# A DiT block, minGRU, Runge-Kutta scan and sparse FFN: the last attention pass by token halves, and the second half's recurrence by time with its later steps on GpSimd

## What is computed

```python
# 1 block: adaLN, 16 heads of 128 (attention inside each sequence of 32 tokens), GELU MLP 256-1024-256
x = x + gate1 * (attention(ln(x) * (1 + scale1) + shift1) @ out_w + out_b)
x = x + gate2 * (gelu((ln(x) * (1 + scale2) + shift2) @ ffn_w1 + b1) @ ffn_w2 + b2)
# 2 minGRU along the 32 tokens of each sequence, in linear form
z = sigmoid(x @ Wz.T + bz); h[t] = (1 - z[t]) * h[t-1] + z[t] * g(x @ Wn.T + bn)[t]; x = x + h
# 3 Runge-Kutta scan, 32 steps, each of four derivatives with tanh(q) @ coupling.T; q starts at cond
# 4 logits = q @ Wr.T; the 4 best of 16 blocks of a 1024-wide hidden layer stay; out = x + W2 gelu(W1 q)
```

## Time and profile before

| | |
|---|---|
| median of 3 runs | 482.5 us (482.31 to 483.1) |
| profiled execution | 482.44 us, of which 480.6 us span from first to last instruction |
| TensorE, weight loads | 467.4 us (97%), 334.8 us (70%) |
| VectorE, ScalarE, GpSimd | 389.3 us (81%), 318.9 us (66%), 48.0 us (10%) |
| chain of work that ended last | TensorE 88%, VectorE 4%, ScalarE 3% |
| last attention pass; LayerNorm 2 to hidden layer | about 176 to 232 us; 232 to 241 us |
| second half's gates to the loop | 291 to 305 us |
| loop | 304.8 to about 469 us |

### The profile page before, as it was taken

One profiled execution on the slowest core, in us unless ns is written; L12 is line 12 of the kernel. 1 busy time (PEld: TensorE's weight loads), 2 busy tenths in 40 slices (PEclk: granted clock), 3 DMA queues, 4 the chain that ended last, 5 costly groups with the idle time before them and its releaser, 6 DMA issues.

```text
span 480.6 us, 13808 instructions
## 1 busy us (share of the span) xinstructions
PE 467.4 (97%) x5271; PEld 334.8 (70%) x5271; DVE 389.3 (81%) x1368; ACT 318.9 (66%) x950; POOL 48.0 (10%) x78
## 2 busy tenths in 40 slices
PE   7999999999999999999899999999999999999997
PEld 4455776557656676568545444788898988989886
DVE  4969895779768899997896997888888888888884
ACT  1677964788477966887476965565665656656563
POOL 3010240223020320223000000000000000000000
PEclk9999999999999999999999999999999999999999
DMA  8992510100201000000000000000000000000000
GB/s 283 419 388 70 135 45 22 62 25 23 66 22 44 22 0 2 0 2 1 1 1 1 0 1 0 3 3 1 0 1 11 12 0 12 0 12 11 1 12 23
DMA packets 10399, 20.85 MB, mean 43 GB/s; under 512 B 1472, under 2 KB 4992, under 8 KB 9728
## 3 DMA queue, kind: packets, MB, share of 16 engines
q1 hardware_dynamic: 9808, 19.89, 12.0%
q10 hardware_dynamic: 560, 0.60, 0.4%
HBM read 19.40 MB, written 1.08 MB: 43 GB/s over the span
## 4 chain that ended last, share of the span: by engine, by line
PE 88%; DVE 4%; ACT 3%; DMA 1%; issue 1%; POOL 1%; SPq 0%; DVEq 0%
PE bank L884 58%; PE score L884 27%; PE spare L884 2%; DMA ao_sb<-xtok 1%; POOL ptx L507 1%; ACT ptx L632 1%; ACT ao_sb L585 1%; DVE drive L1459 1%; ACT x L532 0%; ACT th L810 0%; DVE drive L1463 0%; DVE q_group L2112 0%; DVE tok_stats L1406 0%; DVE acc L1551 0%; DVE drive L1614 0%
## 5 line engine op out<-in xcount | busy, mean ns | idle before, releaser
L884 PE MATMUL bank<-x,pairs_store 128*128 128x512 f16 x384 | 86.3, 379 | 0.5 <-ACT x L532 0.4
L884 PEld LDWEIGHTS bank<-x,pairs_store 128*128 128x128 f16 x384 | 36.9, 98 | 43.4 <-issue 1.4
L507 POOL TENSOR_TENSOR ptx<-pt,ptx 32x256 f16<-32x256 f32 x62 | 43.2, 697 | 176.2 <-ACT ptx L632 172.8
L884 PE MATMUL score<-cub,neg_eye 128*128 128x64 f32 x256 | 55.6, 299 | 0.0
L585 ACT ACTIVATE big<-bank,head_b 128x512 f16<-128x512 f32 x60 | 39.8, 685 | 17.4 <-PE bank L884 17.0
L2026 DVE TENSOR_TENSOR thlo<-th 128x64 f16<-128x64 f32 x128 | 28.8, 225 | 26.0 <-ACT th L811 24.8
L884 PE MATMUL score<-th,coup_part 128*128 128x32 f16 x1024 | 46.2, 177 | 0.9
L884 PE MATMUL bank<-pairs_store,ao_sb 128*128 128x256 f16 x360 | 43.0, 273 | 0.7 <-issue 0.2
L884 PE MATMUL bank<-pairs_store,x 128*128 128x512 f16 x192 | 43.4, 379 | 0.0
L810 ACT ACTIVATE th<-score 128x64 f16<-128x64 f32 x96 | 21.5, 224 | 31.7 <-PE score L884 28.9
L884 PEld LDWEIGHTS bank<-pairs_store,ao_sb 128*128 128x128 f16 x360 | 34.0, 98 | 7.5 <-DVE ao_sb L1652 1.5
(11 more groups left out here) (252 smaller groups left out, 1052.1 us busy)
## 6 DMA issues: line engine op xcount, KB each, us to landing
wqk_sb<-wqk SPq DMA_DIRECT2D x16, 256.0 KB, 2.7
wv_sb<-wv SPq DMA_DIRECT2D x4, 512.0 KB, 5.4
wo_sb<-wo SPq DMA_DIRECT2D x4, 512.0 KB, 4.2
f_sb<-ffn_w SPq DMA_DIRECT2D x2, 1024.0 KB, 14.7
ao_sb<-xtok SPq DMA_DIRECT2D x4, 256.0 KB, 5.8
x_sb<-xT SPq DMA_DIRECT2D x1, 1024.0 KB, 12.5
w_sb<-w1T SPq DMA_DIRECT2D x1, 1024.0 KB, 16.1
w_sb<-w2T SPq DMA_DIRECT2D x1, 1024.0 KB, 16.9
```

Source lines behind the costliest of these rows:

```text
L507: nc.gpsimd.tensor_tensor(ptx[s, 1, :, s], pt[s], ptx[s, 0, :, s], ALU.subtract).then_inc(ptx_ready, 1)
L884: return nc.tensor.matmul(dst, lhsT, rhs, start=start, stop=stop, **kw)
```

## The change

In the last pass the fourth head's softmax, placing and mixing are done per half of the tokens (`half_strips`, `shift_half`, `normalise_half`, `place_high_half`, `mix_half`, on 128 x 128 values each), and TensorE's order becomes: mix_half(2, 0), mix_half(2, 1), (0, 2), mix_half(3, 0), head 2 for c = 0, 1, the SHIFT2 product, head 3 for c = 0, 1, mix_half(3, 1), (0, 3). The heads 2 and 3 for c = 2, 3 come behind `turn_normed(0)`. The unread matmuls there become 4. Because of it `take_heads(2)` and `take_heads(3)` come later in VectorE's stream, `empty_x2(0)` later in ScalarE's, and the banks of the hidden layer's tiles are dealt out anew.

For the second half the time steps are cut into 0 to 7 (EARLY, 128 columns) and 8 to 31 (LATE, 384 columns). VectorE runs the recurrence of the early steps for both ob ahead of the loop. GpSimd computes the late steps' terms (`late_terms`), VectorE scans them in eight pieces of 96 columns in the slots of stages 6 to 13 of iteration 0, and GpSimd adds x and makes the drive pair (`late_pair`). ScalarE makes the late gates of ob = 1 (`late_gates(1)`) just ahead of the loop. 18 unread matmuls become 4, and the sum on TensorE is gone.

The diff, cut to its core:

```diff
 # GpSimd
+                    if i == NQUAD - 1 and j == QUAD - 1:
+                        for h in range(NH):
+                            gs = slice(h * G // 2, (h + 1) * G // 2)
...
+                                nc.gpsimd.tensor_tensor(ptx[s, 1, gs, s], pt[s, gs], ptx[s, 0, gs, s], ALU.subtract
+                                                        ).then_inc(half_placed[h], 1)
-            nc.gpsimd.memset(unit_row, 1.0 / CSCALE).then_inc(unit_ready, 1)
+            def late_terms(ob):
+                z, cand, pos, keep = (late_store[:, ob, w] for w in range(4))
+                use = USE_GRU[1] + ob
+                pool.wait_ge(free[bank_of(use)], count_of(use) + 1)
+                own.step(nc.gpsimd.tensor_scalar(keep, z, -0.5, 0.5, ALU.mult, ALU.add))
+                own.step(nc.gpsimd.tensor_scalar(z, z, 1.0, 0.25, ALU.add, ALU.mult))
+                pool.wait_ge(late_tanh, ob + 1)
+                own.step(nc.gpsimd.tensor_scalar(cand, cand, 0.0, 1.0, ALU.min, ALU.add))
+                use = USE_GRU[1] + 3 - ob
+                pool.wait_ge(free[bank_of(use)], count_of(use) + 1)
+                own.step(nc.gpsimd.tensor_tensor(cand, cand, pos, ALU.add))
+                own.step(nc.gpsimd.tensor_tensor(cand, cand, z, ALU.mult))
+                pool.wait_ge(z_used, KB + ob + 1)
...
+                own.step(nc.gpsimd.tensor_tensor(carry[:, ob], keep, state, ALU.mult))
+                own.step(nc.gpsimd.tensor_tensor(cand, cand, carry[:, ob], ALU.add))
+                nc.gpsimd.memset(keep, 0.0).then_inc(late_ready, 1)
+            def late_pair(ob):
...
+                pool.wait_ge(late_scanned, 4 * (ob + 1))
+                own.step(nc.gpsimd.tensor_tensor(later_steps(drive, ob), steps_of(ob)[:, 2], later_steps(x_sb, ob), ALU.add))
+                own.step(nc.gpsimd.tensor_scalar(shifted_drive, later_steps(drive, ob), c2_shifted[:, ob:ob + 1], None, ALU.add))
+                own.step(nc.gpsimd.tensor_scalar(high, later_steps(drive, ob), c2_shifted[:, ob:ob + 1], None, ALU.add))
+                nc.gpsimd.tensor_tensor(low, shifted_drive, high, ALU.subtract).then_inc(late_split, 1)
 # ScalarE, last pass
+                    copy_half(0)
+                    copy_half(1)
+                    place_high(2)
+                    exps_half(0)
+                    exps_half(1)
+                    place_high_half(0)
+                    empty_pv(2)
+                    empty_pv(3, [0])
+                    place_high_half(1)
+                    mlp_highs(5, 7)
+                    empty_pv(3, [1])
+                    mlp_highs(7, 8)
...
+            act.wait_ge(first_heads_out, 1)
             normalise_x2(0)
+            x1_high(NH)
+            act.wait_ge(last_full, 1)
             empty_x2(0)
-            x1_high(NH)
 # ScalarE, second half
+            early_gates(0)
+            early_gates(1)
+            late_gates(0)
+            drive_bias(2, 3, EARLY)
+            drive_bias(3, 4, EARLY)
             tanh_of(q_group[:, :, UNROLL - 1], Q_UNIT[3])
-            drive_bias(3, 5, slice(0, UNROLL))
-            drive_bias(3, 5, slice(UNROLL, T))
+            late_gates(1)
 # TensorE
+                    mix_half(2, 0)
+                    mix_half(2, 1)
+                    out_project(0, 2, [0, 1])
+                    mix_half(3, 0)
+                    out_project(1, 0, [2])
+                    out_project(1, 1, [2])
+                    pe.wait_ge(ada2_ready, 4)
+                    ada_late(SHIFT2, spare)
+                    out_project(1, 0, [3])
+                    out_project(1, 1, [3])
+                    mix_half(3, 1)
+                    out_project(0, 3, [0, 1])
...
             turn_x2(0)
-            ada_late(SHIFT2, fill(USE_F1[0][3]))
-            unread(score[:, 0], 3)
+            pe.wait_ge(pv_taken, NQUAD * NH)
+            unread(score[:, 0], 4)
             turn_normed(0)
-            unread(fill(USE_F1[0][4])[:], 8)
+            for c in (2, 3):
+                out_project(1, c, [2, 3])
-        USE_F1 = [[AFTER + n for n in (2, 5, 6, 3, 4, 7, 8, 9)], ...
+        USE_F1 = [[AFTER + n for n in (3, 4, 2, 5, 6, 8, 9, 7)], ...
...
+                for ob in range(KB):
+                    early(ob, 1).then_inc(early_full, 1)
+                late(use, wz_sb, 0, 1)
+                for k in range(KB):
+                    late(use + 3, wn_sb, 0, k)
+                pe.wait_ge(early_gate, 3 * KB)
...
+                for k in range(KB):
+                    late(use + 1, wz_sb, 1, k)
+                for k in range(KB):
+                    late(use + 2, wn_sb, 1, k)
-            unread(bank[bank_of(USE_GRU[1] + 1)][:], 18)
+            unread(bank[bank_of(USE_GRU[1])][:], 4)
 # VectorE, last pass
                     low_pv(1, [0])
-                    last_strips(3)
-                    shift(3)
-                    low_pv(1, [1])
-                    normalise(3)
-                    low_pv(2, [0])
-                    add_late(SCALE2, spare, 2, 1.0)
-                    place_last_low()
-                    low_pv(2, [1])
-                    low_last_pv()
+                    half_strips(0)
+                    shift_half(0)
+                    half_strips(1)
+                    shift_half(1)
+                    normalise_half(0)
+                    low_pv(1, [1])
+                    add_late(SCALE2, spare, 2, 1.0)
+                    normalise_half(1)
+                    place_last_low(0)
+                    low_pv(2)
+                    low_last_pv([0])
+                    add_late(SHIFT2, spare, 3)
+                    place_last_low(1)
                     half_var(0)
+                    low_last_pv([1])
             shift_turned(0, 1)
+            take_heads(2)
+            x1_low(0, 1)
             take_heads(3)
-            x1_low(0, 1)
 # VectorE, second half and loop
-            min_gru(2, 2, first_half, (half_ready, 1), (half_ready, 2))
-            min_gru(2, 3, second_half, emptied(use), emptied(use + 1))
-            min_gru(3, 4, every, emptied(use + 2), emptied(use + 3), (za_ready, 1))
-            drive_lows(2, 3, slice(0, UNROLL))
+            for m in range(MB):
+                V.memset(tok_shift[:, m:m + 1], 0.0).then_inc(h_low_ready, 1)
+            for ob in range(KB):
+                early_gru(ob)
+            drive_lows(2, 3, EARLY)
...
+                if n == 0 and slot == 1 and 6 <= at <= 13:
+                    late_scan(at - 6)
+                    return
+                if n == 1 and m == 4:
+                    dve.wait_ge(late_split, KB)
```

More of the change, by code:

```diff
@@ L520, in _ @@
+            for ob in range(KB):
+                late_terms(ob)
+            for ob in range(KB):
+                late_pair(ob)
         @block.scalar
@@ L1085, in out_project @@
                         done.then_inc(filled, uses)
+                    elif last and (pair, c) == (0, 3):
+                        done.then_inc(first_heads_out, 1)
                 values(0, 1)
@@ L1240, in last_gates, with late @@
+                def late(use, weights, ob, k):
+                    dst = fill(use) if k == 0 else bank[bank_of(use)]
+                    last = mm(dst[:, 0:NL], weights[:, k, ob * P:(ob + 1) * P], x3_steps[:, k, NBH:B, LATE], k == 0, k == KB - 1)
+                    if k == KB - 1:
+                        last.then_inc(full[bank_of(use)], 1)
+                use = USE_GRU[1]
                 pe.wait_ge(x3_ready, KB + 1)
-                for c in range(2):
-                    gate(0, c)
-                mm(dst[1][:], wz_sb[:, 0, 0:P], x3[:, 0, HALF:N], True, False)
+                for ob in range(KB):
+                    early(ob, 0)
@@ L1244, in last_gates @@
+                late(use, wz_sb, 0, 0)
                 pe.wait_ge(x3_ready, 2 * KB)
-                gate(1, 0).then_inc(half_full, 1)
-                mm(dst[1][:], wz_sb[:, 1, 0:P], x3[:, 1, HALF:N], False, True).then_inc(full[bank_of(USE_GRU[1] + 1)], 1)
-                gate(1, 1).then_inc(full[bank_of(USE_GRU[1])], 1)
-                for w, weights in enumerate((wn_sb, wz_sb)):
-                    product(USE_GRU[1] + 2 + w, lambda k: weights[:, k, P:2 * P], lambda k: x3[:, k, HALF:N], KB)
+                for ob in range(KB):
+                    early(ob, 1).then_inc(early_full, 1)
@@ L1834, in _ @@
                     root_done(0)
+                    dve.wait_ge(first_heads_out, 1)
                     for g in range(FIRST_G):
@@ L1837, in _ @@
                                         ).then_inc(first_normed, 1)
-                    take_heads(2)
-                assert own.n == STEPS and pairs[0] == (i + 1) * PAIRS + (0 if last else 4)
-            own.n, own.base = start + NQUAD * STEPS, 0
-            add_late(SHIFT2, bank[bank_of(USE_F1[0][3])], 3)
+                assert own.n == STEPS + (4 if last else 0) and pairs[0] == (i + 1) * PAIRS + (0 if last else 4)
+            own.n, own.base = start + NQUAD * STEPS + 4, 0
             dve.wait_ge(ada2_ready, 5)
```

324 lines of the change are left out of this document (208 added, 116 removed).

## The result

| | before | after |
|---|---|---|
| median | 482.65 us (7 runs) | 485.38 us (7 runs, 485.29 to 487.84) |
| ratio | | 1.0076, 95% interval 1.0057 to 1.0095 |
| profiled execution | 482.44 us, span 480.6 | 487.6 us, span 485.8 |
| mean granted clock | 1.00 in the profiled execution until 0.6 us ahead of the span's end | 0.993 in four runs (485.3 to 485.4), 0.986 in three (487.6 to 487.8) |

The change makes the kernel 0.76% slower, where the forecast was 0.4% faster; 485.4 lies above the range (to 483.0). The runs of the changed kernel fall into two groups by their granted clock, and the profiled execution belongs to the slower one.

What follows compares the result with a forecast made beforehand. Two gaps of about 12 us, ahead of the hidden layer and of the loop, were bound by other engines, the rest by TensorE. 482.44 - 0.5 - 2.8 + 1.6 = 480.7 us; range 478.3 to 483.0.

Steps and rivals of the forecast that it cites:

- Part 1: Last attention pass to the hidden layer: -0.7 + 0.4 - 0.2 = -0.5 us, ends -1.2 and +0.5.
- Part 3: In the loop: GpSimd's two-input instructions hold thlo, scans cost 0; +1.6 us, ends 0 and +6.
- Part 2: Way from the second half's x3 to the loop: -4.4 us, with holds of 1.6 giving -2.8.
- the new uses: New bank order of the hidden layer's tiles: take_heads(2)'s bank returns 0.4 us, two spared GELU stalls give 0.2.
- The gain of the heads: Last attention pass: first heads taken at 228.15 instead of 228.96, 0.8 us earlier.
- The walk: Queues followed in the last pass: low strips at 224.3, head 2 on TensorE from 225.1, SHIFT2 product to 227.3.
- the lock: GpSimd reading two SBUF inputs holds VectorE's two-SBUF-input instructions: 1.6 us ahead of the loop, 1.6 in it.
- The price of GpSimd's one-input instructions: GpSimd on 384 columns with one input: 0.45 us each, at 1 ns a column.
- Rival 1: GpSimd runs where VectorE has slack, so holds miss the path: 477.5 us, with half the holds 479; chance 0.14.
- Rival 3: In the loop each of 13 GpSimd instructions holds a chain link: 7.3 us lost, 486.4 in all; chance 0.11.
- Rival 4: Clock falls to 1.2 GHz near 234, 24 matmuls behind take 2.6 us more: 483.3; chance 0.07.
- its point of decision of 4.3: Loss in the loop from which the slower outcome by holds there was to count as decided: 4.3 us.

Runs made afterwards that it cites:

- the kernel with the banks in order: The changed kernel with the first half's last three hidden tiles in banks 3, 4, 0 instead of 4, 0, 3: 484.41 us, ratio 1.0039.
- the memsets: The changed kernel with GpSimd's eleven late-step instructions per feature block replaced by memsets of the same outputs: 480.01 us, ratio 0.9953.
- the first experiment: The changed kernel with 13 unread matmuls instead of 4 between the second half's gates and the loop: 486.76 us, ratio 1.0078.
- the pieces: The kernel before with the second half's change alone, GpSimd's late terms cut into 3 pieces and pair into 4: 484.23 us, ratio 1.0034.
- the terms only: The kernel before with the second half's change alone, late_pair's four GpSimd instructions per feature block as memsets: 482.32 us, ratio 0.9997.

## Why the prediction was wrong

The sum failed in two of its three terms, and a fourth was missing. Part 1 stood at -0.5 and came out at +1.2, because the new banks were not followed to the last tile. Part 3 stood at +1.6 and came out at +3.4, because the holds were sized too small and looked for at thlo only. The clock stood at nothing and took 3.4 us in the profiled execution. Part 2 came out as forecast, at -2.8.

**The sum by measured terms.** Against the profiled execution before (482.44): attention part +0.1 (x3 at 293.06 against 292.93, banks in order), bank +1.1 (294.14 against 293.06), clock at the turning +1.3 (295.44 against 294.14), way to the loop -2.8, scans and waits in the loop +0.6, holds in the loop +2.8, clock in the loop +2.1. That is 487.6, the profiled execution after. The runs at 0.993 had less of the clock's 3.4 us and give 485.4. Without the clock the same sum is 484.2: slower, too. No run of the changed kernel had a full clock, so this is an estimate; the kernel with the banks in order, 1.1 less by the same sum, ran at 483.4 and 483.6 with one.

**Part 1 failed at the sentence on the new uses**, "The new uses also spare two short stalls on GELUs (0.2 in all)". I followed the new banks to the tile that shares one with `take_heads(2)`, and that was right (k = 1 came 4.5 us behind the scaling, as forecast), but did not follow the last three tiles: the permutation puts the last tile where the output layer begins. It costs 1.1 to 1.2 us where I had a gain of 0.2. **The gain of the heads was a size:** forecast 0.8, measured 0.24 (0.45 and 0.32 in the two kernels with the attention part alone). The walk was right up to the low strips (forecast 224.3, measured 224.05); then TensorE reached head 2 at 225.50 instead of 225.1, waiting for VectorE's low parts (row 225.50 above), and the SHIFT2 product ended about 0.5 late. In the kernel with the attention part alone and the banks in order the scaling came 0.24 earlier (236.99 against 237.23), `take_heads(2)`'s bank took 0.4 as forecast, and x3 was 0.1 late; with the last tile's bank that makes +1.2.

**Part 2 was right in both terms, the second partly by luck.** Without a lock the way shortens by 12.74 - 8.25 = 4.5 us (forecast 4.4); the lock takes 1.67 (forecast 1.6). The place was partly another: I had it in the two-input instructions of early_gru(1). One of these was held (301.49, 0.95 us against 0.29 for its form alone), but more lies in the drive pair's low half, held for 0.75 us, and two holds of 0.3 come from one-input instructions (rows 299.23 and 299.67, beside L552 and L554). What I had left out and what didn't reach the path made up for one another.

**Part 3 had the right mechanism and mis-sized it.** "one meets thlo with chance 0.65 and holds it 0.4 on average: 0.26 each, 1.6 in all", for six two-input instructions: in the kernel with the banks in order five thlo are long, by 0.29, 0.47, 0.57, 0.25 and 0.90 us, together 2.5. Three of them belong to two-input instructions, 1.9 us in all; fewer than the four I had counted, but longer, since the subtraction that writes the low half takes 1.97 us, not my 0.95. The other two, 0.5 us, belong to one-input instructions, which I had left to the range. And thlo is not the only link: beside GpSimd's subtraction of 322.23 one of the eight scans took 1.22 us instead of 0.35, the linear term (L2345) stood behind it in VectorE's stream, and TensorE waited 0.76 us for that term:

```profile
322.67 1.22 DVE L2149 TENSOR_TENSOR_SCAN big<-big 128x96 f32<-128x96 f32 x1
```

```profile
324.08 0.23 PE L995 MATMUL score<-drive_pair,scaled_eye 128*128 x2 [0.76 <-DVE score L2345]
```

In these two iterations TensorE waited 2.4 us for thlo and 1.0 for L2345, about the 3.44 that they are longer; with memsets it waited 0.4 for VectorE. "Eight scans of 0.36 replace eight split pieces of similar length: 0" was 0.6, and the scans brought a second link that GpSimd can hold.

**The price of GpSimd's one-input instructions** ("0.45 with one") held for two of the forms (0.53 to 0.54), while three took 1.25, 1.50 and 2.66. That cost less than it looks: a thlo that started inside the 2.66 us instruction took 0.23 as always (in the kernel with the banks in order it started at 321.10, under 319.50 to 322.15), and in the changed kernel one at 306.08, inside the 1.50 us instruction, took 0.21.

```profile
319.50 2.65 POOL L580 TENSOR_SCALAR drive_pair<-drive,c_shifted 128x384 f16<-128x384 f32 x1
```

```profile
321.10 0.23 DVE L2236 TENSOR_TENSOR thlo<-th 128x64 f16<-128x64 f32 x1
```

The Trainium skill (SBUF — State Buffer, "Who interferes with whom") states that the second one is fully blocked. The trace agrees nearly for the two-input instructions (thlo of 331.61, held until 1.53 us into an instruction of 1.95), and not for the late part of the long one-input ones.

**The rivals.** Rival 1 fell: the holds reach the path. Rival 3's mechanism is what happened in the loop, at 2.8 instead of 7.3 us. The loop lost 5.5 in all, above its point of decision of 4.3, but 2.1 of that is the clock and 0.6 the scans and waits. Rival 4's is what happened at 234.50, and cost half of the 2.6 I had priced; it happened in four of the profiled executions with the new attention part (the changed kernel, its loop filled, the banks in order, the memsets) and not in the three others that left the turning as it was. I had weighed the clock at one place only, where TensorE would be left with four unread matmuls, and with 0.07. The larger part of it came in the loop, which I had counted as TensorE's own work.

What brings the clock down in the loop is open in part. That it comes with GpSimd's computing is shown: with memsets the second half alone kept 0.999 or 1.0 in all four runs, and with GpSimd computing it ran below that in five of six, in all ten with the pieces and in nine of ten with the terms only. That the holds do it, through TensorE's waits, is argued and not shown. For it: the falls in iteration 1 come 0.7 us behind a wait of 0.85 (changed kernel) and 1.7 us behind one of 0.89 (pieces). Against it: with the banks in order the same waits left the loop at a full clock, and the pieces, with less waiting for thlo, had a mean below 0.999 in every run. The pause ahead of the loop isn't needed, by the first experiment and by the pieces, which have none of 2 us there; but four profiled executions fell 0.1 to 2.5 us behind that pause, and the memsets take it away too. Nor does a mean of 0.996 need GpSimd's late work: the kernel before had one such run of 21 (484.71 us) among those measured beside the second half's. Why executions of the same kernel differ was not settled. TensorE's pauses in the loop are single waits of at most 0.9 us, also where the clock fell with the gap ahead of it filled. The Trainium skill (TensorE: Matmul & The Clock Gate, "HAM oscillation — how this bites in real kernels") has pauses inside a kernel bring the clock down.

**Not tried:** to give thlo's subtraction one operand in the matmuls' banks, so that it might not meet GpSimd. The kernel's banks (five numbered, two of `score`, `spare`) all have users, so one would have to be freed first.

## What to carry to other kernels

When banks are dealt out anew, follow each one to its next user, the last tile above all: a permutation that looks like bookkeeping cost 1.1 us, and the reordering that it served gained nothing. Before work is moved to GpSimd beside a serial loop, look whether a VectorE instruction with two SBUF inputs lies on that loop's chain or ahead of a link in VectorE's stream; if so, what moves is paid by holds. Here these plus the clock took back 5.1 to 6.8 us of a kernel that was 4.3 us faster without them. The same kernel with memsets in GpSimd's place is a cheap bound: it shows what the shorter way is worth when nothing is held.

## What the runs showed of the hardware that was not expected

- The loop can lose its full clock though TensorE is busy for 22.36 of 24.41 us in the iteration and no single wait in it is longer than 0.9 us: the level of 1.2 GHz stood from 306.18 to 313.01 us in iteration 0, and in the changed kernel with banks in order and pieces from 325.06 to 335.30. It differs between executions of the same kernel (483.18 at 1.0 against 485.2 at 0.989), so one profile does not give a kernel's time here.
- GpSimd's instructions of 128 x 384 float32 cost by form: multiply and add by constants 0.53 to 0.54 us, minimum and add 1.50, adding a per-partition column 1.25, the same with a strided float16 output 2.66; two inputs 1.00, with the strided float16 output 1.97. A memset of this size took 0.42, of the strided float16 output 1.84.
- GpSimd's two-input instructions held thlo for most of what was left of them (until 1.53 us into one of 1.95), the long one-input ones only in a part of it, and a memset of 1.84 us not at all.
- Not only subtractions of two SBUF tiles were held: a scan of 96 columns took 1.22 instead of 0.35 us, and under GpSimd's work in pieces of 0.70 us a clip took 1.01 instead of about 0.2, longer than one piece.
